# Perceiver block on one core: K and V projection units interleaved with context units, attended halves summed in the transpose, tail and last value units as fp32 matmuls

## What is computed

```python
q = einsum('bsd,ed->bse', x, wq)                       # 8 x 64 x 1024
k = concatenate([ctx, einsum('bsd,ed->bse', x, wk)])   # 1601 context rows + 64 new rows
v = concatenate([ctx, einsum('bsd,ed->bse', x, wv)])   # the same context rows are keys and values
attn = softmax(q @ k.T / 32)                           # 64 x 1665 for each batch
x = x + (attn @ v) @ wo.T
x = x + self_attention(layernorm(x))                   # 16 heads, rotary, causal
x = x + mixture_of_experts(layernorm(x))               # 8 experts, routed
```

## Time and profile before

| | |
|---|---|
| median of 3 runs | 1362.84 us (1360.22 to 1364.38) |
| the profiled execution | 1364.01 us, span 1362.2 us |
| PE busy | 1239.1 us, 91% |
| DVE busy | 855.8 us, 63% |
| ACT busy | 629.5 us, 46% |
| granted TensorE clock, mean | 0.95 |
| DMA | 278.10 MB, mean 204 GB/s |
| L743, the low parts | 240 instructions, 537.6 us on DVE |
| L501, the high parts | 240 instructions, 450.4 us on ACT |

### The profile page before, as it was taken

The page is one execution under the profiler, slowest core; times in us unless marked ns, Lnnn a source line. Parts: engine busy times, 40 slices in busy tenths (PEclk is TensorE's granted clock), DMA queues, the critical chain, the costliest instruction groups (busy, mean ns, idle before and its releaser), DMA issues.

```text
span 1362.2 us, 19335 instructions
## 1 busy us (share of the span) xinstructions
PE 1239.1 (91%) x7542; PEld 1073.5 (79%) x7542; DVE 855.8 (63%) x978; ACT 629.5 (46%) x559; POOL 95.4 (7%) x82
## 2 busy tenths in 40 slices
PE   4999978787878699999999489999999999999995
PEld 3888756566656478888888489999999999999894
DVE  7333588999999856664646565565656564646460
ACT  4111477777778642312442144444444535454431
POOL 0000000000000000000000001111111111111101
PEclk7999988989998899999999599999999999999998
DMA  8234489999999981422232335757565767666632
GB/s 307 83 140 137 154 320 306 326 348 324 338 337 329 315 311 74 180 102 82 79 118 109 130 133 200 219 199 216 213 200 204 213 216 210 221 189 242 177 133 32
DMA packets 68047, 278.10 MB, mean 204 GB/s; under 512 B 22072, under 2 KB 22216, under 8 KB 45344
## 3 DMA queue, kind: packets, MB, share of 16 engines
q1 hardware_dynamic: 57312, 245.58, 52.1%
q0 software_dynamic: 10688, 31.87, 8.1%
HBM read 258.55 MB, written 18.87 MB: 204 GB/s over the span
## 4 chain that ended last, share of the span: by engine, by line
PE 72%; DVE 10%; DMA 9%; issue 4%; ACT 3%; SPq 0%; POOL 0%; DVEq 0%; ACTq 0%; POOLq 0%
PE ps L1212 22%; PE ps L1214 22%; PE ps L1213 22%; DVE lo L743 6%; DMA raw<-context 4%; ACT hi L501 3%; DMA raw<-new_values 2%; DMA raw<-keys 2%; PE ps L1369 1%; PE ps L1570 1%; PE ps L1308 1%; DVE cols L827 1%; PE ps L1434 1%; PE ps L1226 1%; DVE attended L866 1%
## 5 line engine op out<-in xcount | busy, mean ns | idle before, releaser
L743 DVE TENSOR_TENSOR lo<-raw,hi 128x2048 fp32r<-128x2048 f32 (+1 forms) x240 | 537.6, 2252 | 185.9 <-ACT hi L501 184.2
L501 ACT ACTIVATE hi<-raw 128x2048 fp32r<-128x2048 f32 (+1 forms) x240 | 450.4, 1885 | 342.1 <-PE ps L1214 270.7
L1212 PE MATMUL ps<-act_hi,hi 128*128 128x256 f32 (+1 forms) x1152 | 341.5, 296 | 6.8 <-DVE act_lo L766 4.8
L1214 PE MATMUL ps<-act_hi,lo 128*128 128x256 f32 (+1 forms) x1152 | 340.5, 296 | 0.0
L1213 PE MATMUL ps<-act_hi,hi 128*128 128x256 f32 x1024 | 289.7, 283 | 0.0
L1212 PEld LDWEIGHTS ps<-act_hi,hi 128*128 128x128 f32 x1152 | 221.2, 192 | 13.0 <-DVE act_lo L766 5.2
L1214 PEld LDWEIGHTS ps<-act_hi,lo 128*128 128x128 f32 x1152 | 221.1, 192 | 5.3
L1213 PEld LDWEIGHTS ps<-act_hi,hi 128*128 128x128 f32 x1024 | 196.6, 192 | 0.3
L1212 PE MATMUL ps<-hi,act_hi 128*128 128x512 f32 x384 | 151.9, 396 | 0.0
L1214 PE MATMUL ps<-hi,act_lo 128*128 128x512 f32 x384 | 150.2, 391 | 0.0
L1213 PE MATMUL ps<-lo,act_hi 128*128 128x512 f32 x384 | 150.1, 391 | 0.0
(11 more groups left out here) (189 smaller groups left out, 1268.4 us busy)
## 6 DMA issues: line engine op xcount, KB each, us to landing
raw<-weights SPq DMA_DIRECT2D x128, 1024.0 KB
raw<-keys SPq DMA_DIRECT2D x48, 1024.0 KB
raw<-context SPq DMA_DIRECT2D x48, 1024.0 KB
raw<-key_tail SPq DMA_DIRECT2D x8, 264.0 KB
raw<-context SPq DMA_DIRECT2D x8, 260.0 KB
xq<-x_in SPq DMA_DIRECT2D x4, 512.0 KB, 5.6
new_keys_t<-kvs POOLq DMA_DIRECT2D x8, 256.0 KB, 3.1
new_values<-kvs POOLq DMA_DIRECT2D x8, 256.0 KB, 2.7
```

The source lines that it names most:

```text
L501: act.activation(part(hi, k, kind), part(raw, k, kind), ACT.Copy).then_inc(hi_done, 1)
L743: dve.tensor_tensor(part(lo, k, kind), part(raw, k, kind), part(hi, k, kind), ALU.subtract).then_inc(lo_done, 1)
L1212: pe.matmul(out, a_hi, b_hi, start=first, stop=False)
L1214: return pe.matmul(out, a_lo, b_hi, start=False, stop=last)
```

## The change

The order of units from the ninth place of the program on is new, and the attention steps are written out without a loop.

- **Order.** Wq as before. Then four groups of one Wk unit and three key units (batches 0 and 1). Then 20 units: Wv 0, tails of batches 0 and 1, Wv 1, four key units of batch 2, Wv 2, the last two key units and the tail of batch 2, the first value unit of batch 0, Wv 3, the other value units of batch 0. Step s (1 to 5) then has the keys of batch s+2 and the values of batch s; steps 6 and 7 have values alone.
- **Wv units** hold a quarter of the columns for all rows: each is 4 tiles x 8 chunks x 3 matmuls of 256 columns, with 4 outputs in turn in two PSUM banks. Output n waits for the copy of output n-2. Wk units too have two banks, with two outputs each.
- **Plain units.** The tail unit and the last value unit are no longer split. TensorE reads `raw` in fp32, so SP's load of unit k+4 waits until TensorE has used unit k. The value rows' low part for chunk 11 is moved behind the last unit, so the last value unit also releases `lo` of the unit before it.
- **Attended rows.** ACT scales both halves on their way out (`o_out`, one instruction of 128 x 1024), with the inverse sum spread over both halves by a small matmul; `turn_o` multiplies by `fold`, two identities one above the other, which adds the halves.
- `pt` has two buffers, and the transposes of the weights of batch s+1 stand after the third value unit of step s.

In the diff below `load` and the loads are SP's, `o_out` is ACT's, `v_out`, the loop over 20 units and `step` are DVE's, `v_unit` and `tail_unit` are TensorE's, and the last piece is from TensorE's `value_unit_pe`. `load_tail(0)` waits for all eight stores of new keys before it loads the new ones, and `load_last(0)` for all sixteen stores of new values. `split` does nothing for a plain unit. ACT's lists have the same form as DVE's: in the 20 units `tail_copy(0)` and `tail_copy(1)` follow the splits at r = 1 and 2 and `exps` those at r = 3 and 13; in a step `exps` follows the split at pos 8, `pt_hi` that at pos 10, and `o_out(s)` stands at the end.

```diff
 def load(k, src, per=0, i=0, dst=None):
-    if k >= RING:
-        sp.wait_ge(lo_done, k - RING + 1 + per * i)
+    if k >= RING and k - RING in PLAIN:
+        name, value = free[k - RING]
+        sp.wait_ge(release[name], value)
+    elif k >= RING:
+        sp.wait_ge(lo_done, splits(k - RING) + per * i)
...
+load(V_UNIT[0], w_d[8])
+load_tail(0)
+load_tail(1)
+load(V_UNIT[1], w_d[9])
+for u in range(4):
+    load_keys(2, u)
+load(V_UNIT[2], w_d[10])
...
+def o_out(s):
+    act.wait_ge(o_ready, s + 1)
+    act.wait_ge(rinv_ready, s + 1)
+    act.activation(O[:, :], ps[:, PV_BANK:PV_BANK + 2, :].rearrange("p a n -> p (a n)"), ACT.Copy,
+                   scale=rinv[:, s % 2:s % 2 + 1]).then_inc(o_norm, 1)
...
+def v_out(m):
+    for n in range(TT * m, TT * m + TT):
+        dve.wait_ge(out_ready, O_V + n + 1)
+        dve.wait_ge(kv_stored[n % 2], 16 * (4 + n // 2))
+        dve.tensor_copy(kvs[:, n % 2, 0:D // 4], ps[:, PROJ_BANK + n % 2, 0:D // 4]).then_inc(evacuated, 1)
...
+for r in range(20):
+    split(U_B + r + AHEAD)
+    if r == 0:
+        q_lo(2)
+        v_out(0)
+    elif r == 3:
+        row_max(0)
+        row_max(1)
+        v_out(1)
+    elif r == 4:
+        pt_lo(0)
+    elif r == 5:
+        score_add(2, 0)
+    elif r == 7:
+        score_add(2, 1)
+    elif r == 8:
+        q_lo(3)
+        v_out(2)
+    elif r == 10:
+        score_add(2, 2)
+    elif r == 12:
+        row_max(2)
+    elif r == 13:
+        v_out(3)
+    elif r == 16:
+        pt_lo(1)
...
+def step(s):
+    keys = s + 2 < B
+    for pos in range(0 if keys else 7, PER_STEP):
+        split((key_unit(s + 2, pos) if pos < 7 else value_unit(s, pos - 7)) + AHEAD)
+        if pos in (1, 3, 5):
+            score_add(s + 2, pos // 2)
+        if pos == (2 if keys else 8):
+            ot_lo(s - 1)
+        if pos == 4 and s + 3 < B:
+            q_lo(s + 3)
+        if pos == 7 and keys:
+            row_max(s + 2)
+        if pos == 10 and s + 1 < B:
+            pt_lo(s + 1)
...
+def v_unit(m):
+    k = V_UNIT[m]
+    unit_ready(k)
+    for t in range(TT):
+        n = TT * m + t
+        pe.wait_ge(evacuated, O_V + n - 1)
+        if n in (4, 5):
+            pe.wait_ge(tail_done, n - 3)
...
+def tail_unit(s):
...
+    for c in range(C):
+        ins = pe.matmul(ps[0:QL, 3 if s == 1 else TAIL_BANK, 0:KEYS - KFULL], q[:, s, c, :],
+                        view[:, c, 1:KTAIL + QL], start=(c == 0), stop=(c == C - 1))
+    ins.then_inc(tail_ready, 1)
...
+        if u == 6:
+            n = QL if j else KREM
+            pe.matmul(ps[0:QL, PV_BANK + h, :], ptl[0:n, s % 2, j, :], raw[0:n, k % RING, at],
+                      start=False, stop=False)
+            if j == 1:
+                ins = pe.matmul(ps[:, PV_BANK + h, :], pt[:, s % 2, NCH - 1, :],
+                                lo[:, (k - 1) % RING, at], start=False, stop=True)
```

More of the change, by code:

```diff
@@ L89, in by_tile @@
                 unit("out_ready", base + 4 * (g + 1))
[L91 to L100, removed]
+    for k in range(U_WO):
+        unit(*marks.get(k, (None, 0)))
     by_tile(O_WO)
@@ L180, in perceiver_block @@
         landed = [sem(f"landed{s}") for s in range(RING)]
-        new_landed = sem("new_landed")
+        new_landed = [sem(f"new_landed{s}") for s in range(2)]
         hi_done = sem("hi_done")
@@ L609, in _ @@
+            for s in range(1, B):
+                step(s)
             split(U_WO + 3)
-            ot_hi(7, 7)
+            ot_hi(7)
             split(U_QKV)
@@ L876, in _ @@
-            q_lo(0, 0)
-            q_lo(1, 1)
-            for pos in range(7):
-                split(U_KEYS0 + pos + AHEAD, kind=KEY_LAST if pos + AHEAD == 6 else None)
-                if pos in (1, 3, 5):
-                    score_add(0, pos // 2)
-                if pos == 6:
-                    score_add(0, 3)
-            row_max(0)
-            step(0)
-            with dve.Fori(0, 3) as i:
-                steps.loop(i, 4)
-                step(1, i, True)
-                step(2, i, True)
-                steps.end(3)
@@ L892, in _ @@
+            for s in range(1, B):
+                step(s)
             split(U_WO + 3)
-            ot_lo(7, 7)
+            ot_lo(7)
             def add(base, out, bank, g, t):
@@ L1281, in _ @@
             pe.wait_ge(ln_lo, 2 * TT)
-            for k in range(2 * RING):
+            for k in range(RING):
                 def bank_free(j):
@@ new lines, in _, with step @@
+            value_unit_pe(0, 1)
+            value_unit_pe(0, 2)
+            turn_p(1)
+            for u in range(3, 7):
+                value_unit_pe(0, u)
+            def step(s):
+                keys = s + 2 < B
+                if keys:
+                    score_unit(s + 2, 0)
+                    score_unit(s + 2, 1)
+                    turn_o(s - 1)
+                    for u in range(2, 6):
+                        score_unit(s + 2, u)
+                    tail_unit(s + 2)
+                for u in range(7):
+                    value_unit_pe(s, u)
+                    if u == 0 and not keys:
+                        turn_o(s - 1)
+                    if u == 2 and s + 1 < B:
+                        turn_p(s + 1)
@@ L1384, in _ @@
+            for s in range(1, B):
+                step(s)
             pe.wait_ge(ot_split, B - 2)
-            pe.wait_ge(s_evac, 4 * B)
+            pe.wait_ge(s_evac, 3 * B)
+            pe.wait_ge(tail_done, B)
             for t in range(TT):
```

622 lines of the change are left out of this document (336 added, 286 removed).

## The result

The changed kernel takes 1381.49 us (median of 4 runs, 1380.75 to 1384.53), the kernel before 1363.06 in the runs beside it (4 runs, 1360.22 to 1364.38). The ratio is 1.015, 95% interval 1.0128 to 1.0173: slower, by 18 us. The profiled execution took 1384.53 us, the longest of the four, with a span of 1382.6.

A forecast was written before the change was run, and what follows sets the result against it. TensorE bounded projections; attention steps were held by the four slots' round trip, neither DMA nor DVE at its limit. 248.8 + 5 x 41.5 + 2 x 20.1, plus 0.3, put Wo 4.5 us later: 1367 us, range 1347 to 1384.

The forecast's parts named there:

- last units at half clock: Rival: each step's last unit runs at half clock after TensorE waits, 3.4 us each, 1377 to 1391 us; chance 0.18.
- the likeliest case: The forecast holding as made, 1367 us, own range 1358 to 1376; chance 0.50.
- a Wo anywhere but near 497: Sign of being wrong: first Wo matmul not starting near 497 us; forecast 496.8 against 492.3 before.
- Wk groups: Four groups of one Wk unit and three key units: no stall, 16.35 us each, Wk 3 ending at 131.4.
- Wv stalls: Twenty units with Wv: TensorE idles 21.5 us for DVE copies, plus 10.5 us at half clock; Wv 3 ends at 234.5.
- A step: Attention steps with keys and values: 41.5 us each instead of 40.9, bounds 39.5 and 45.
- The last two steps: Steps 6 and 7, values without keys: 20.1 us each, counted from load landings, the value unit and the fp32 last unit.
- The sum: All stages up to Wo: 496.5 us and 0.3 for larger constants, Wo 4.5 us later, kernel 1367 us.
- The fp32 price: Last value unit in plain fp32: 0.85 us per 512-column matmul, 3.9 us a unit in place of 1.85.
- copies are not held back: Rival: DVE gets to the Wv output copies in time, 32 us less, 1335 us; chance 0.10.
- The fp32 unit costs 2.3: Rival: plain last value unit at the bound from below, 12.8 us less over 8 units, 1354 us; chance 0.12.
- The clock stays up: Rival: no half clock through the Wv waits, 10.5 us less, 1356.5 us; chance 0.10.

The follow-up runs named there:

- the first experiment: Changed kernel with DVE and ACT lists reordered in the twenty units with Wv, copies ahead of splits and row_max: 1362.18 us, ratio to before 0.9993.
- the last experiment: Changed kernel with `o_out` on ACT ahead of the split beside the last value unit in steps 5 to 7: 1395.05 us, ratio 1.0207.
- the fastest one: Changed kernel with copies first, last units and tails of batches 3 to 7 split, four store buffers, earlier `o_out` in steps 5 to 7: 1344.20 us.
- the exponential: Changed kernel with row_max and the exponential of a step moved behind the splits of the fifth and sixth value units: 1386.69 us, ratio 1.0188.

## Why the prediction was right, and where it was wrong

The forecast was 1367 us, slower as the likeliest sign, with a range to 1384; 1381.5 is in the range and slower, but outside the likeliest case's own range of 1358 to 1376. The range reached to 1384 because of a rival, last units at half clock, that holds for one last unit only, so that the number lies in it is in part luck. The prediction also named as a sign of being wrong a Wo anywhere but near 497, and it is at 514.2. By the milestones of the profiled execution, in order:

- **Wk groups: right.** No stall; Wk 3 ends at 132.1, its last copy starts at 132.30, against 131.4.
- **Wv stalls: right in place and nearly in size, and in part luck.** The third Wv output waits for a copy that stands behind a split: forecast 5.7, 6.2 and 6.2 us, measured 6.7, 4.8 and 6.1; behind `tail_copy(1)` 2.4 forecast, 2.3 measured. Idle in all 21.5 forecast, 19.95 measured. Half clock behind each: forecast, seen, and gone with the waits in the first experiment. Its cost was put at 10.5 us and is 7.3, the 80.75 us of busy time of this stretch less the 73.48 of the same work at full clock in the first experiment. The work itself was put at 71.1 us and is these 73.5. So 71.1 + 21.5 + 10.5 = 103.1 us stand against 73.5 + 19.95 + 7.3 = 100.7, from an end of Wk 3 that came 0.7 later: Wv 3 ended at 232.8 against 234.5. `o_out` of batch 0 is at 249.8, after ACT's 1.9 us split that stands ahead of it; the unit's end is 0.9 before the forecast 248.8. What I had not seen is DVE's store wait of 4.96 us in Wv 2, and it cost nothing.
- **A step: the term that was mis-sized.** "I take 41.5 for 40.9 now": measured 43.9 on average, 12.2 us in five steps. In the step of the chain above two terms are off: the last unit has 4.6 us instead of 3.9, and the sixth value unit is ready 1.2 us later, behind loads that land late. And another of the five steps (293.27 to 341.44, 48.2 us) had its last unit at half clock. There the four pieces of the unit took 5.50, 0.72, 1.90 and 0.74 us, as in the chain of the last experiment.

- **The last two steps: mis-sized.** 20.1 each forecast, 46.6 together measured, 6.4 more. By the chain they are two waits of 3.11 us for `o_norm` and 40.4 us of TensorE's work, with the clock at 0.50 behind each wait; the forecast had neither, and went by the loads. That way is as long, as the last experiment shows, because "4.9 + 2 x 2.55" let two more full loads land 2.55 us apart. ACT's timeline above has its high parts, each at a landing, at 472.52, 476.34 and 480.64 for a plain unit that ended at 467.63: 4.9, 8.7 and 13.0 us, so 3.8 and 4.3 apart, with the small pieces of a last unit queued behind. That those pieces are the cause is my reading and not shown.
- **The sum.** Wo at 514.2 instead of 496.8: 17.4 later, which is -0.9 at the end of batch 0, +12.2, +6.4, and -0.3 for larger constants that I had added and that did not show. From Wo on 1.5 us less.

The fp32 price came from a slope over narrow matmuls: 0.427 us a record, and it was 0.477, so 12% short; the bound from below, 2.3 us a unit, is ruled out. The Trainium skill's Perfetto Trace Analysis, section Engine Utilization, divides the array's rate by 2 for FP32_LOW_HIGH; this trace has 0.95 us for a matmul of 512 columns, four times the 0.23 of an fp32r one, so that division can't be the whole price of an fp32 product. For a single record it agrees: 0.477 us is twice the 0.23.

Of the rivals, *copies are not held back* is false for this kernel, but it names the repair: with the order turned round the copies were nearly in time, worth 19 us and not 32. *The fp32 unit costs 2.3* is false. *The clock stays up* is false. *The last unit at half clock* is true of one last unit in eight here, short of its own mark. What the forecast said of balance was wrong in one place: it had the relief of DVE and the held slot nearly cancel in a step. The relief is worth nothing measurable (the kernel before with the attended rows alone), and the plain units cost 24 us in all, some 15 of them for the last units, in the steps, and some 8 to 9 for the tails, in the twenty units with Wv. And that the loads are not at their limit in a step, as the prediction says, isn't settled: in the kernel before, in those with the last unit split and with both split, and in the fastest one, the step is 40.3 to 41.4 us long, and the DMA share is 0.96 or 0.97 each time.

## What to carry to other kernels

Interleaving independent work pays only if every in-order list keeps its hand-over copies ahead of anything that waits for a load: the same units cost 19 us more with a PSUM copy behind a split. With the copies first, the last units split, all tails but the first three split, four store buffers and `o_out` earlier in the last steps, the interleaved order beats the kernel before by 1.5%. An operand that TensorE reads straight from its landing slot saves instructions on engines that have slack, and holds the slot through its use; price the loads that queue behind that slot, not the instructions spared. The price depends on what stands behind those loads: the plain tails cost 8 us where copies wait behind splits, and those of the first three batches save 5.8 us once the copies come first. Before taking an idle stretch off the chain, ask when the next operand would be ready without it: twice here (the exponential, the attended rows) the wait only moved to the next load.

## What the runs showed of the hardware that was not expected

- In step 6 of the changed kernel 1 MB loads in one queue, with the small pieces of a last unit behind them, land 3.8 to 4.3 us apart at a DMA share of 1.0 (1.01 to 1.04 from 471.6 to 483.6 us), not 2.5 apart as in the earlier trace rows. By the landing records of the trace, of the sixteen parts of the two late loads (476.3 and 480.6 us) fifteen were in 1.3 and 2.7 us before the last one; why one part lags stays open.
- An fp32 matmul of 512 columns is two records of 0.477 us at full clock (2.86 us for six) and of 0.92 at half clock (5.50 for six).
- A store of new values (128 KB) issued while loads ran held its copy back by 6.83 us; the longest of that kernel took 7.6 us from issue to landing, the median 2.1.
